# Sliding-window attention: values one group later, statistics behind the next maxima, rotations first on GpSimd

## What is computed

```python
qkv = hidden_states @ Wqkv
q, k, v = jnp.split(qkv, 3, axis=-1)
q = rope(rmsnorm(q, q_norm_w)); k = rope(rmsnorm(k, k_norm_w))
mask = (q_idx >= k_idx) & (q_idx - k_idx <= WINDOW - 1)
scores = einsum('bqhd,bkhd->bhqk', q, k) * scale        # masked with -inf
o = einsum('bhqk,bkhd->bqhd', softmax(scores), v)
x = _layernorm(x + o @ Wo)
x = _layernorm(x + ffn(x))      # shared expert and top 2 of 8 experts
```

## Time and profile before

| | us |
|---|---|
| three runs | 1092.43, 1090.77, 1092.11 |
| median | 1092.11 |
| profiled execution, its own time | 1092.02 |
| its span, first to last instruction | 1090.2 |
| attention, up to the first matmul of the second half | about 424 |
| PE busy in the span | 1034.2 (95%) |
| DVE, ACT, POOL busy | 766.5, 639.6, 447.0 |

### The profile page before, as it was taken

One profiled execution on the slowest core, in us unless ns is written; L12 is line 12 of the kernel. 1 busy time (PEld: TensorE's weight loads), 2 busy tenths in 40 slices (PEclk: granted clock), 3 DMA queues, 4 the chain that ended last, 5 costly groups with the idle time before them and its releaser, 6 DMA issues.

```text
span 1090.2 us, 19793 instructions
## 1 busy us (share of the span) xinstructions
PE 1034.2 (95%) x7116; PEld 851.0 (78%) x7116; DVE 766.5 (70%) x1165; ACT 639.6 (59%) x1301; POOL 447.0 (41%) x548
## 2 busy tenths in 40 slices
PE   5799999999999977999999999999999999999995
PEld 3577777777777754887888888888888888887884
DVE  4888777787877864775676677767666777674573
ACT  3566666666666554334666666666666666664353
POOL 4677887777788730001122222222222222221271
PEclk8999999999999996899999999999999999999998
DMA  6111111111111103357798999999999999995552
GB/s 204 33 51 32 32 32 31 32 45 49 32 32 32 31 30 108 119 188 235 241 259 245 253 281 256 262 242 276 249 275 255 259 267 259 265 235 133 160 196 89
DMA packets 121265, 171.88 MB, mean 158 GB/s; under 512 B 10144, under 2 KB 63776, under 8 KB 121088
## 3 DMA queue, kind: packets, MB, share of 16 engines
q1 hardware_dynamic: 112432, 150.16, 43.6%
q0 software_dynamic: 8736, 20.45, 11.6%
HBM read 151.97 MB, written 23.07 MB: 161 GB/s over the span
## 4 chain that ended last, share of the span: by engine, by line
PE 58%; DVE 1%; ACT 1%; issue 0%; DMA 0%; POOL 0%; ACTq 0%; POOLq 0%; DVEq 0%
PE up_ps L1359 4%; PE up_ps L1360 4%; PE up_ps L1358 4%; PE gate_ps L1358 4%; PE gate_ps L1359 4%; PE gate_ps L1360 4%; PE down_ps L1385 3%; PE down_ps L1384 3%; PE down_ps L1383 3%; PE e_up_ps L1409 3%; PE e_up_ps L1410 2%; PE e_up_ps L1411 2%; PE e_up_ps L1420 2%; PE e_up_ps L1418 2%; PE e_up_ps L1419 2%; PE e_gate_ps L1418 2%
## 5 line engine op out<-in xcount | busy, mean ns | idle before, releaser
L902 POOL DMA_INDIRECT sum_dram<-rows,target_i x39 | 62.8, 1609 | 365.7 <-ACT rows L1002 365.7
L1230 DVE TENSOR_TENSOR e_lo<-e_raw,e_hi 128x1408 fp32r<-128x1408 f32 x78 | 126.6, 1624 | 47.9 <-ACT e_hi L976 47.9
L976 ACT CAST e_hi<-e_raw 128x1408 fp32r<-128x1408 f32 x78 | 107.5, 1380 | 55.0 <-PE e_up_ps L1420 55.0
L317 ACT ACTIVATE prob<-score_ps,nbias 128x256 f32<-128x256 f32 x256 | 119.5, 476 | 8.9 <-DVE nbias L413 8.6
L257 POOL TENSOR_TENSOR probT<-probT,masks 128x256 f32<-128x256 f32 x128 | 97.2, 781 | 64.6 <-DVE probT L434 64.6
L1235 DVE TENSOR_TENSOR ed_lo<-ed_raw,ed_hi 128x1024 fp32r<-128x1024 f32 x39 | 47.8, 1225 | 71.8 <-ACT ed_hi L984 46.3
L908 POOL DMA_INDIRECT rows<-x_dram,token_i x39 | 53.1, 1363 | 99.7 <-DVE target_i L1199 70.4
L413 DVE TENSOR_REDUCE nbias<-score_ps 128x2 f32<-128x512 f32 x128 | 88.5, 691 | 4.4
L325 ACT COPY probT<-probT_ps 128x512 f32<-128x512 f32 x64 | 37.5, 587 | 91.2 <-PE probT_ps L541 91.2
L507 PE MATMUL proj_ps<-wqkv_lo,xT_hi 128*128 128x512 f32 x180 | 78.7, 437 | 0.0
L509 PE MATMUL proj_ps<-wqkv_hi,xT_lo 128*128 128x512 f32 x180 | 71.3, 396 | 0.0
(11 more groups left out here) (230 smaller groups left out, 2949.1 us busy)
## 6 DMA issues: line engine op xcount, KB each, us to landing
e_raw<-in_We_gu SPq DMA_DIRECT2D x78, 704.0 KB
ed_raw<-in_We_down SPq DMA_DIRECT2D x39, 512.0 KB, 5.4
raw_ring<-in_Ws_gu SPq DMA_DIRECT2D x58, 256.0 KB
wd_raw<-in_Ws_down SPq DMA_DIRECT2D x44, 256.0 KB, 6.7
gu_raw<-in_Ws_gu SPq DMA_DIRECT2D x30, 256.0 KB
ed_raw<-in_We_down SPq DMA_DIRECT2D x39, 192.0 KB, 6.8
xT_in<-in_xT SPq DMA_DIRECT2D x16, 256.0 KB, 2.8
x_in<-in_x SPq DMA_DIRECT2D x16, 256.0 KB, 3.7
```

The source lines that it names most:

```text
L317: nc.scalar.activation(prob[:, g % 2, h, :], score_ps[:, h, 0:2 * P], ACT.Exp, bias=nbias[:, s % 2, head:head + 1], scale=1.0, accum_out=r ...
L976: nc.scalar.copy(e_hi[:, half * HK:(half + 1) * HK, :], raw_half(i, half)).then_inc(e_hi_made, 1)
L1230: nc.vector.tensor_tensor(e_lo[:, part, :], raw_half(i, half), e_hi[:, part, :].bitcast(FP32), ALU.subtract).then_inc(e_lo_made, 1)
```

## The change

1. `probT` is doubled (index n % 2). Each step ends with `values(n - 1)` in place of `values(n)`; the copies and masks for group n wait for `pv_mm` n - 1, and no longer for POOL's reads. `steps()` has one more block.
2. All that depends on complete values of block s - 1 moves a group back: the product oT and its high and low parts to g = 2, the wo projection to g = 3, and v's projection and copy to g = 2 in exchange. `res` stands at the end of g = 3; its statistics and the reciprocal root stand in g = 0 of the next block, `x1` in g = 1, its transposition in g = 0 of the block behind that; the transposition of `spread` in g = 1.
3. On DVE, reciprocal, spread and statistics stand behind the maxima of group 0, not in front.
4. On POOL, each rotation is done whole, and in front of the masks of its step; the reciprocal root stands in g = 0, in front of the key copies.

```diff
-        probT = sb("probT", [P, 4, 3, P])
+        probT = sb("probT", [P, 2, 4, 3, P])
...
-            return [(s, g) for s in range(-1, NB + 2) for g in range(GROUPS)]
+            return [(s, g) for s in range(-1, NB + 3) for g in range(GROUPS)]
```

GpSimd, `own_part` and its steps:

```diff
-                    wait(pool, pv_mm, n)
+                    wait(pool, pv_mm, n - 1)
...
                 if g == 1 and has(a):
...
                         rotate_cos(pool, nc.gpsimd, a, 0, rot_a[:, :], q_cs, q_weighted, q_part)
+                        rotate_sin(pool, nc.gpsimd, a, 0, rot_a[:, :], rot_b[:, :], q_part, q_rot)
                 if g == 2 and has(a):
...
                     scale_trig(pool, nc.gpsimd, a, 1, k_rms, k_cs)
+                    wait(pool, q_rot, a + 1)
+                    rotate_cos(pool, nc.gpsimd, a, 1, rot_a[:, :], k_cs, k_weighted, k_part)
+                    rotate_sin(pool, nc.gpsimd, a, 1, rot_a[:, :], rot_b[:, :], k_part, k_rot)
                 if has(n // 4):
                     own_part(n)
                 if g == 0:
                     if has(s):
                         v_difference(s)
+                    if has(s - 2):
+                        wait(pool, mv_made, s - 1)
+                        nc.gpsimd.tensor_scalar(rstd[:, 1:2], mv[:, 1:2], 1.0, LN_EPS, ALU.mult, ALU.add).then_inc(ln_var, 1)
+                        wait(pool, ln_var, s - 1)
+                        nc.gpsimd.tensor_tensor(rstd[:, 0:1], rstd[:, 1:2], half[:, :], ALU.pow).then_inc(ln_rstd, 1)
                     copy_keys(s)
-                if g == 1 and has(a) and a:
-                    rotate_sin(pool, nc.gpsimd, a, 0, rot_a[:, :], rot_b[:, :], q_part, q_rot)
```

ScalarE (VectorE's copy of probT changes in the same way):

```diff
-                wait(act, pv_mm, n)
-                wait(act, own_made, 2 * n)
+                wait(act, pv_mm, n - 1)
...
-                if g == 0 and has(s - 1):
+                if g == 1 and has(s - 1):
                     wait(act, rrep_mm, s)
...
-                if g == (3 if s >= 0 else 2) and has(a):
+                if g == 2 and has(a):
                     wait(act, v_mm, a + 1)
```

VectorE:

```diff
-                if g == 1 and has(s - 1):
+                if g == 2 and has(s - 1):
                     wait(dve, pv_mm, 4 * s)
                     wait(dve, rrep_made, s)
...
                 if has(s):
                     masked_max(s, g, 1)
+                if g == 0 and has(s - 1):
+                    wait(dve, exp_made, NH * s)
+                    nc.vector.reciprocal(rinv[:, :], rsum[:, (s - 1) % 2, :]).then_inc(rinv_made, 1)
...
+                if g == 0 and has(s - 2):
+                    wait(dve, res_made, s - 1)
+                    nc.vector.bn_stats(bn6[:, :], res[:, :]).then_inc(bn_made, 1)
...
+                if g == 1 and has(s - 2):
+                    wait(dve, ln_rstd, s - 1)
...
+                if g == 3 and has(s + 2):
+                    split_xT(s + 2)
+                if g == 3 and has(s - 1):
                     wait(dve, wo_mm, s)
                     wait(dve, x1_made, s - 1)
```

TensorE:

```diff
                 if g == 0 and has(a):
                     wait(pe, xT_lo_made, a + 1)
                     wait(pe, v_made, a)
+                    wait(pe, res_made, s - 1)
...
-                if g == 2 and has(s - 1):
+                if g == 2 and has(a):
                     wait(pe, k_sq, min(a + 1, NB))
+                    part, done = (x_hi, x_lo, wqkv_hi, wqkv_lo, 2), v_mm
+                if g == 3 and has(s - 1):
+                    wait(pe, v_made, min(a + 1, NB))
                     wait(pe, oT_lo_made, s)
...
-                if g == 0 and has(s - 1):
+                if g == 0 and has(s - 3):
+                    wait(pe, x1_made, s - 2)
+                    turned(x1[:, (s - 3) % 2, :]).then_inc(x1T_mm, 1)
+                if g == 1 and has(s - 1):
                     wait(pe, rinv_spread, s)
                     turned(spread).then_inc(rrep_mm, 1)
...
-                if behind:
-                    values(n)
+                if has((n - 1) // 4):
+                    values(n - 1)
```

More of the change, by code:

```diff
@@ L322, in probT_out @@
                 wait(act, probT_mm, 2 * n + 2)
[L323 to L325 removed]
+                wait(act, pv_mm, n - 1)
+                nc.scalar.copy(probT[:, n % 2, 2:4, 0:2, :], probT_ps[1][:, 0, :].rearrange("p (h w t) -> p h w t", h=2, w=2)).then_inc(probT_act, 1)
             def split_xT(b):
@@ L357, in _ @@
                     nc.scalar.copy(oT[:, :], turned_ps[:, 0, :]).then_inc(rrep_made, 1)
-                if g == 1 and has(s - 2):
-                    wait(act, x1T_mm, s - 1)
-                    nc.scalar.copy(x1T[:, :, (s - 2) * P:(s - 1) * P], tiled(turned_ps[:, 0, :])).then_inc(x1T_made, 1)
+                if g == 0 and has(s - 3):
+                    wait(act, x1T_mm, s - 2)
+                    nc.scalar.copy(x1T[:, :, (s - 3) * P:(s - 2) * P], tiled(turned_ps[:, 0, :])).then_inc(x1T_made, 1)
                 if g == 2 and has(a):
@@ L443, in _ @@
                 a, n = s + 1, 4 * s + g - 1
-                if g == 0 and has(s - 1):
-                    wait(dve, exp_made, NH * s)
-                    nc.vector.reciprocal(rinv[:, :], rsum[:, (s - 1) % 2, :]).then_inc(rinv_made, 1)
-                    wait(dve, rinv_made, s)
-                    nc.vector.tensor_copy(spread[:, :].rearrange("p (h d) -> p h d", d=HD), rinv[:, :].unsqueeze(2).to_broadcast([P, NH, HD])).then_inc(rinv_spread, 1)
-                if g == 1 and has(s - 1):
+                if g == 2 and has(s - 1):
                     wait(dve, pv_mm, 4 * s)
@@ L458, in _ @@
                     masked_max(s, g, 1)
+                if g == 0 and has(s - 1):
+                    wait(dve, exp_made, NH * s)
+                    nc.vector.reciprocal(rinv[:, :], rsum[:, (s - 1) % 2, :]).then_inc(rinv_made, 1)
+                    wait(dve, rinv_made, s)
+                    nc.vector.tensor_copy(spread[:, :].rearrange("p (h d) -> p h d", d=HD), rinv[:, :].unsqueeze(2).to_broadcast([P, NH, HD])).then_inc(rinv_spread, 1)
+                if g == 0 and has(s - 2):
+                    wait(dve, res_made, s - 1)
+                    nc.vector.bn_stats(bn6[:, :], res[:, :]).then_inc(bn_made, 1)
+                    wait(dve, bn_made, s - 1)
+                    nc.vector.bn_aggr(mv[:, :], bn6[:, :]).then_inc(mv_made, 1)
+                if g == 1 and has(s - 2):
+                    wait(dve, ln_rstd, s - 1)
+                    wait(dve, x1_stored, 16 * (s - 3))
+                    wait(dve, x1T_mm, s - 3)
+                    nc.vector.tensor_scalar(x1[:, s % 2, :], res[:, :], mv[:, 0:1], rstd[:, 0:1], ALU.subtract, ALU.mult).then_inc(x1_made, 1)
                 if s == 0:
                     split_wo(g)
-                if g == 1 and has(s - 1):
+                if g == 2 and has(s - 1):
                     wait(dve, oT_hi_made, s)
@@ L608, in _ @@
                     part, done = (oT_hi, oT_lo, wo_hi, wo_lo, 0), wo_mm
-                if g == (3 if s >= 0 else 2) and has(a):
-                    wait(pe, res_made, s)
-                    part, done = (x_hi, x_lo, wqkv_hi, wqkv_lo, 2), v_mm
                 if part and not first:
```

41 lines of the change are left out of this document (7 added, 34 removed).

## The result

The changed kernel takes 1083.8 us (median of 6, 1079.95 to 1086.26) against 1091.92 (1090.77 to 1094.13) before: 0.9918 times, with an interval of 0.990 to 0.9936. So it is faster by 0.8%, where I had forecast 1087.0. (The ratio and its interval come from means of the runs; the two medians alone give 0.9926.) The profiled execution took 1084.33 with a span of 1082.5.

A forecast was written before the change was run, and what follows sets the result against it. PE bounds blocks 2 to 14, so only its idle time, mainly the wait for Pool's masks, can be won. -6.2 + 1.9 - 0.7 - 0.9 + 0.8 = -5.1 us from 1092.02 gives 1086.9, shown as 1087.0; range 1083.0 to 1090.2.

The forecast's parts named there:

- Direction and main mechanism: Blocks 2 to 14, group 1: values a group later remove PE's wait for Pool's masks, 13 x 0.48 = -6.2 us.
- k's rotation late by 0.3 in six blocks: Group 3 of key-copying blocks 4, 5, 8, 9, 12, 13: PE waits 0.3 us each, +1.9, bounds 0 and +3.6.
- meetings: DVE's spread, norm product and oT_lo running beside Pool's work: each delays Pool 0.44 us, 3 x 0.44 = 1.3 per key-copying block.
- Rival A: Whole kernel: no meetings cost anything and the tail keeps its clock, -8.3 us, 1083.8; chance 0.20.
- B: Loop's key-copying blocks: meetings cost their upper bound, +3.6; whole change -3.2 us, 1088.9; chance 0.20.
- C: Group 3: k's rotation becomes the gate in every block, at most +29, a third taken: 1095 us; chance 0.07.
- D: Group 1: the masks' wait is replaced by an equal one on exponentials or squares, no effect, 1091.5 us; chance 0.11.
- First blocks: Blocks 0 and 1 (28.7 to 76.9 us): fewer Pool waits, -0.7 us, bounds +0.3 and -2.
- Block 15: Last block: groups 0 and 1 give 0.25 each, group 2's projection moves to group 3; -0.9 us, bounds -0.3 and -1.2.
- Behind block 15: Last transposes to last oT: two values products instead of one, at half clock, +0.8 us, bounds -0.5 and +1.2.
- Second half: From 430 us on: untouched, moves as a whole with the loop's gain or loss; no term of its own.

The follow-up runs named there:

- pad2: Changed kernel plus two unused power instructions on GpSimd in front of q's chain in every block: 1097.27 us, ratio 1.0043.
- pad1: Changed kernel plus one unused power instruction on GpSimd in front of q's chain in every block: 1088.64 us, ratio 0.9971.
- stats_front: Changed kernel with DVE's reciprocal, spread, statistics and aggregate moved ahead of the first maxima of group 0: 1098.21 us, ratio 1.0058.
- v_block0: Changed kernel with v's projection of block 1 back in group 3 of block 0: 1084.3 us, ratio 0.9935.
- v_block0b: Changed kernel with v of block 1 again projected in group 3 of block 0, second profile and runs: 1084.4 us, ratio 0.9926.
- masks_first: Kernel before the change, with Pool's two masks in group 1 put ahead of q's whole rotation: 1097.79 us, ratio 1.0055.
- rot_first: Kernel before the change with only Pool's new order, each rotation whole and ahead of its masks: 1157.32 us, ratio 1.060.
- control: Changed kernel unaltered, run and profiled again: 1084.98 us, ratio 0.9936.
- control2: Changed kernel unaltered, a third profile and five rounds: 1083.92 us, ratio 0.9926.
- pool_old: Changed kernel with Pool's old order, sine parts and k's rotation behind the masks again: 1094.57 us, ratio 1.0022.

## Why the prediction was right or wrong

**Direction and main mechanism: right.** Values a group later took the masks' wait away in blocks 2 to 14 and no lower limit came: 13 x 0.48 = 6.2 forecast, 6.5 found. The rest is in block 2, whose group 0 lasts 5.35 since it has no `x1` to turn; I had not counted that.

**k's rotation late by 0.3 in six blocks: wrong, and this is the step that failed.** The +1.9 did not come: PE waits for k's rotation in no block. The count without meetings was 2.0 into group 3; the trace has 2.81, where PE wants 3.06; I had 3.3. Two things differ from my sum, one by less and one by more:

- The price of a meeting for Pool. I took 3 x 0.44 = 1.3 from oT_lo and the masks in the earlier trace rows. In block 8 the spread cost Pool 0.17 (`v_step` 1.47 for 1.30) and the norm product 0.18 (0.92 for 0.74), and oT_lo next to nothing (`cs_rms` 0.36 for 0.32): 0.35 in all. The loser was DVE: the norm product took 1.26 for 0.54, and nobody waited for that.
- The working around them made 0.46 more than my rounded numbers: 0.19 ahead of q's chain, 0.12 at the masks and 0.27 in k's chain, less 0.12 in q's. In k's chain it is mostly the gap behind the scaling of the table (L168): its start is 0.49 ahead of the cosine part's (231.94 to 232.43), where before masks followed it after 0.28 (209.88 to 210.16). 2.0 + 0.35 + 0.46 = 2.81.

That oT_lo costs next to nothing is not peculiar to block 8. It starts 3.56 us into group 2 in block 8 and in block 7 alike. In block 8 the key copies have made Pool late, so Pool's cosine part starts 1.0 behind it, at 232.43, after it has ended. In block 7, without copies, it is the pair that I had feared, and DVE and Pool both lose:

```profile
208.17 1.29 POOL L176 TENSOR_TENSOR rot_a<-qk,cs_rms 128x512 f32<-128x512 f32 x1
209.40 1.19 POOL L184 TENSOR_TENSOR rot_b<-qk,cs_rms 128x256 f32<-128x256 f32 x1
```

```profile
208.26 1.75 DVE L469 TENSOR_TENSOR oT_lo<-oT,oT_hi 128x512 fp32r<-128x512 f32 x1
```

There Pool loses 0.45 and has 0.91 left. So the 0.44 was the right price of that meeting, but it falls in the blocks that can pay it: oT_lo took 0.68 in all six blocks that copy keys and 1.75 to 1.79 in six of the seven others. I had not foreseen that, so it was luck for the change and no merit of the forecast.

The Trainium skill (SBUF - State Buffer, Who interferes with whom) names both cases, a two-port `copy` or `tensor_scalar` and an operation with two SBUF inputs, and says "Issue order, not op shape, decides who blocks." The traces agree: the norm product, issued at 225.63 behind Pool's 225.31, ended at 226.89, 0.3 behind the end of the cosine part (226.60). I used the rule as if Pool lost each time. It never said so.

Rival A's term for the loop (no loss by meetings) is what came, though its reason, that meetings cost Pool nothing, did not: they cost 0.35 to 0.8 and fitted into the room. The pads show how narrow this was: 0.25 us of room, and 0.65 more work cost 4.7. A's number for the whole, 1083.8, is the measured median to the tenth, and that is luck: its -0.7 for the first blocks was +1.2, its -0.5 behind block 15 was +0.1, and the -1.3 of the second half and -0.4 of the start stood in no sum.

**Rivals B, C and D: no.** None of PE's waits in the loop is left. C's mechanism is real, since pad2 reached eleven blocks and 12.7 us, but needs 1.3 us more on Pool than the change brings.

**First blocks: -0.7 forecast, +1.2 in the profile.** I had looked at group 2 of block 0, which got v's projection, and not at group 3, which lost it. There PE now idles 1.49 and 1.54 us, and the clock falls to half, the level of 1.2 GHz, just behind it:

```profile
49.01 0.66 PE L510 MATMUL probT_ps<-ident,qk 128*128 128x128 f32 x4 [1.49 <-DVE probT L430]
...
51.99 0.69 PE L524 MATMUL score_ps<-kT_lo,qT_hi 32*128 32x384 f32 x4 [1.54 <-issue]
```

```profile
52.00:56.00 4.00, 4.00 (x23) 3.37 (x24) 3.03 (x7) 0.74 (x2) 0.35 (x1) 0.50 0.37 91
```

The first group of block 1 took 8.07 for it. The profile of pad1, whose PE stream is the same, has the same idle time (PE busy 2.96 of 6.00 from 46 to 52) and no fall, 5.49 for that group and 47.23 for both blocks:

```profile
52.00:56.00 4.00, 4.00 (x31) 3.08 (x24) 3.53 (x8) 1.61 (x5) 1.18 (x2) 1.00 0.46 123
```

With the clock kept the stage gives -1.0, near the forecast. What I missed is that this stage can lose 2.2 us by the clock. Does the new idle time invite the fall? Of the seven profiles with that group empty, five had a clock of 0.50 or 0.57 from 52 to 56 us and two kept 1.00 (pad1, stats_front). With its projection in place, the kernel before and v_block0 kept 1.00, while v_block0b, masks_first and rot_first had 0.71 to 0.78 from 46 to 52. So the fall comes with and without it. Whether it is deeper or more frequent in the changed kernel stays open.

**Block 15: -0.9 forecast, -0.8 found.** The split was wrong. Its groups start at 378.44, 382.46, 387.19 and 391.40, so they last 4.0, 4.7, 4.2 and, with the projection that group 2 lost, 6.65.

**Behind block 15: +0.8 forecast, +0.1 found.** From the last prob transposes to the last oT it is 4.71 (398.05 to 402.76) against 4.97 in the earlier trace rows. I had priced PE's two values products at half clock. The clock held until the last oT, and fell only then:

```profile
398.05:402.76 4.71, 3.92 (x68) 2.88 (x64) 3.00 (x7) 1.76 (x3) 2.34 (x4) 1.00 0.21 59
402.76:410.00 7.24, 5.03 (x16) 3.78 (x16) 1.92 (x4) 0.62 (x1) 0.00 (x0) 0.76 0.10 36
```

Before, the first of these stretches (404.53 to 409.50) had 0.56. Just ahead of it PE had waited 2.40 us for the masks before the change (until 403.74); now no wait from 393 to 402 is longer than 0.35. So at this clock the step costs nothing, as I had written for full clock, and gives 0.26; that the removed 2.4 us wait kept the clock up fits, but no run tested it. Behind oT 0.4 came back, half of it a longer wait for the router's weights (3.7 for 3.5).

**Second half: nothing forecast, -1.3 found.** The same instructions run there. The difference is in its start, cut at the same distance from the first gate matmul (423.80 and 430.16). The kernel before ran its second ten microseconds at 0.88:

```profile
440.16:450.16 10.00, 10.00 (x40) 8.11 (x40) 7.13 (x57) 4.50 (x5) 0.00 (x0) 0.88 0.18 53
```

and the changed one at 1.00:

```profile
433.80:443.80 10.00, 10.00 (x48) 8.32 (x47) 8.41 (x57) 5.52 (x7) 0.00 (x0) 1.00 0.18 53
```

The difference arises in its first 18 us: the first product into `down_ps` (L1380 of the changed kernel) starts 17.83 into it before and 16.25 now, 1.6 earlier, and the two keep that distance up to 98 us. In the profiles of control, control2, v_block0 and v_block0b the second half takes 658.4 to 659.9, in pool_old, pad1 and pad2 660.1 to 660.2, in rot_first 656.6. This is spread, which a forecast should carry as width and not as a term.

**The sum.** -0.4 + 1.2 - 6.5 - 0.8 + 0.1 - 1.3 = -7.7 in the profiled execution, -8.1 in the medians. Beyond the forecast of -5.1 this is 2.6: 1.9 by the late rotation that did not come, 1.3 by the second half, 0.7 by the clock behind block 15 and 0.7 by the start and block 2, less 1.9 in the first blocks and 0.1 in block 15. My range had width for the meetings and hardly any for the clock at its lower end: it ended at 1083.0, the median lies 0.8 inside, and two of the six times (1079.95 and 1081.01) lie below it.

## What to carry to other kernels

When an operation on a busy helper engine is late, look for a consumer that can take its result a group later before reordering the helper: reordering alone moved the wait to the next group (+4.2 us in the loop here) or made it longer where it stood (+58.6), while later consumption gave it the room to be reordered. Before pricing a contention, lay the two engines' starts side by side in the order to come. Here that order decided which engine lost and in which blocks, and the longest losses, on DVE, fell where nobody waited for it. If the margin that is left is some tenths of a us, pad the chain by a known amount: here that showed in one run where the margin lay and in which blocks.

## What the runs showed of the hardware

- GpSimd's instructions on one column are not free: 0.19 us for the `tensor_scalar` and 0.55 for the power; from its start to that of the next dependent instruction 0.27 and 0.65. The two for the norm took 0.87 us of a chain with 0.25 to spare.
- In the changed kernel the same DVE product took 0.55 us undisturbed and up to 1.29 beside GpSimd, which itself lost 0.18; in blocks 2 to 14 oT_lo took 0.68 to 1.79, with a loss of up to 0.45 for GpSimd. From block 3 on the pattern repeats over the blocks by their number modulo 4. In the list of one line (count, least, median and most in ns):

```profile
L464 DVE TENSOR_SCALAR x<-res,mv,rstd x16: 546/941/1293, 86.6 to 412.0; 128x512 f32<-128x512 f32 x16
```

- TensorE's clock is not given by the instructions alone. With the same instructions of PE in that stage, the clock of 52 to 56 us was 0.50 in one profile and 1.00 in another, worth 2.2 us. A stage with idle time on PE has this spread; blocks 2 to 14, without idle time, repeated within 0.1 us.
- Waits of 3.1 us a block went with a greater loss than themselves: in rot_first's blocks 2 to 14, 40.4 us of waits, at a mean clock of 0.93, went with 58.6 us of loss.
